# The last attention layer of a graph network: one-hot products from rows kept on chip in place of a scatter, with its output blocks issued by SyncE

## The reference

```python
h = (x @ W).reshape(n, H, C)                       # H = 2 heads of C = 64
a_s = einsum('nhc,hc->nh', h, att_src); a_d = einsum('nhc,hc->nh', h, att_dst)
e = leaky_relu(a_s[s] + a_d[d], 0.2)               # s, d: the edges, then a loop for each node
p = exp(e - segment_max(e, d)[d])
alpha = p / (segment_sum(p, d)[d] + 1e-16)
out = segment_sum(h[s] * alpha[:, :, None], d) + b
h_out = out + x @ Wsk2 + bsk2                      # then the outer residual and layernorm
```

## Time and profile before

| what | us |
|---|---|
| median of 3 runs | 6690.39 (6684.87 to 6695.83) |
| span of the profiled execution | 5389.4 |
| what lies around the span (median less span) | 1301.0 |
| the stages from the first instruction of e4g to the end | about 897 |

### The profile page before, as it was taken

The page is one execution under the profiler, slowest core; times in us unless marked ns, Lnnn a source line. Parts: engine busy times, 40 slices in busy tenths (PEclk is TensorE's granted clock), DMA queues, the critical chain, the costliest instruction groups (busy, mean ns, idle before and its releaser), DMA issues. The chain is left out here.

```text
span 5389.4 us, 98297 instructions
## 1 busy us (share of the span) xinstructions
PE 3527.9 (65%) x21061; PEld 2451.3 (45%) x21062; DVE 3341.7 (62%) x13740; ACT 2224.4 (41%) x6490; POOL 3612.4 (67%) x4923
## 2 busy tenths in 40 slices
PE   4447798777688699969599999520009994100398
PEld 3437687767566344412166666410007773100133
DVE  6454587444388576778488888623518886153388
ACT  0015476767577344423278888300004441000155
POOL 2767577767545677637488888675755556757698
PEclk8669999999899899979799999755559996555699
DMA  1015598989999611101134444341129985311498
GB/s 43 1 56 159 173 281 249 264 245 262 216 279 278 245 53 53 46 17 38 51 124 141 142 142 142 115 122 34 41 81 291 290 290 159 83 32 41 153 343 299
DMA packets 574488, 817.78 MB, mean 152 GB/s; under 512 B 143654, under 2 KB 291021, under 8 KB 573858
## 3 DMA queue, kind: packets, MB, share of 16 engines
q1 hardware_dynamic: 419372, 557.29, 33.3%
q0 software_dynamic: 69184, 122.90, 9.2%
q10 hardware_dynamic: 85784, 136.02, 6.7%
HBM read 494.99 MB, written 329.46 MB: 153 GB/s over the span
## 5 line engine op out<-in xcount | busy, mean ns | idle before, releaser
L619 POOL DMA_INDIRECT agg_dst<-e_rows,e_put_i x392 | 390.6, 996 | 204.3 <-issue 118.8
L1889 POOL DMA_INDIRECT e_rows<-h,e_other_i x392 | 389.2, 993 | 150.9 <-issue 118.9
L1219 POOL TENSOR_TENSOR n_rstd<-n_rstd,minus_half 128x4 f32<-128x4 f32 x294 | 333.5, 1134 | 23.1
L688 POOL DMA_INDIRECT agg<-e_msg,e_put_i x196 | 195.0, 995 | 166.3 <-DVEq L717 115.0
L1232 ACT ACTIVATE n_o<-n_y_ps,n_shift,n_rstd 128x128 f32<-128x128 f32 x784 | 293.6, 458 | 14.8 <-POOL n_shift L1502 13.7
L365 POOL DMA_INDIRECT by_src<-s_pay_s,s_place_i x196 | 189.1, 965 | 114.0 <-issue 58.9
L2388 POOL TENSOR_TENSOR n_u<-n_u 128x512 f32<-128x512 f32 x98 | 124.5, 1271 | 205.8 <-DVE n_u L2335 205.8
L905 POOL DMA_INDIRECT x_rows<-x,d_other_i x196 | 185.8, 948 | 86.1 <-issue 58.8
L2189 PE MATMUL n_y_ps<-n_w,n_gt 128*128 128x128 f32 x1568 | 240.4, 276 | 0.0
L1712 POOL DMA_INDIRECT lg_rows<-x,e_other_i x196 | 186.4, 951 | 78.0 <-issue 59.4
L1113 PE MATMUL e_xl_ps<-gat_wl,e_xg 128*128 128x512 f32 x392 | 225.1, 657 | 18.0 <-ACT e_xg L1086 18.0
(11 more groups left out here) (510 smaller groups left out, 11771.4 us busy)
## 6 DMA issues: line engine op xcount, KB each, us to landing
n_ag<-agg_dst SPq DMA_DIRECT2D x294, 264.0 KB, 3.9
n_hs<-h SPq DMA_DIRECT2D x196, 264.0 KB
n_xs<-x SPq DMA_DIRECT2D x196, 256.0 KB, 4.3
agg_dst<-e_ev SPq DMA_DIRECT2D x196, 132.0 KB
y<-n_o ACTq DMA_DIRECT2D x98, 264.0 KB, 3.6
e1a_fed<-y SPq DMA_DIRECT2D x196, 132.0 KB
m<-e1a_ev SPq DMA_DIRECT2D x196, 132.0 KB
e1b_fed<-m SPq DMA_DIRECT2D x196, 132.0 KB
```

The lines of the kernel that those rows point to most:

```text
L619: pool.indirect_dma_start(out=agg, out_offset=bass.IndirectOffsetOnAxis(ap=e.put_i[:, c:c + 1], axis=0), in_=rows[:, c, :], in_offset=None ...
L688: pool.indirect_dma_start(out=agg, out_offset=bass.IndirectOffsetOnAxis(ap=e.put_i[:, c:c + 1], axis=0), in_=msg[:, g % SLOTS, k, 0:out_wi ...
L1219: st(pool.tensor_tensor(rstd, rstd, keep.minus_half[:, :], ALU.pow))
L1889: pool.indirect_dma_start(out=rows[:, c, :], out_offset=None, in_=h, in_offset=bass.IndirectOffsetOnAxis(ap=e.other_i[:, c:c + 1], axis=0))\
```

## The change

Only the last attention layer changes; the one before it (`e3`, `n3`) keeps its form. `a4` now holds `a_s` and `a_d` (four values for each node), `s4` is 132 wide with ones in the last four columns, and the tables of `walk_tables` are kept to the end. `gat_edges` and `node_last` give way to `edge_shares` and `walk_last`.

`edge_shares` gathers as before, while TensorE and VectorE find four values of each edge's target (its own logit for two heads, and `a_d` for two). The gathered `a_s` is then added by TensorE, in edge order. `softmax` includes the self loop for each edge, and makes for each edge its final share and, for the last edge of a target, the target's own share less one. These go through HBM into edge order; the own share replaces columns 128 and 129 of the edge's row. There is no scatter and no `agg_dst`.

`walk_last` multiplies the rows by their shares (VectorE, 49 operations), and then walks the 396 steps; GpSimd makes the one-hot matrices. A block's two tiles start from `s4` (ScalarE), columns 0 to 127 collect the result and columns 128 and 129 the own share. When a block's steps are done (`close`, on SyncE), VectorE multiplies `h4` by the own share, adds the sums and takes the statistics; ScalarE takes the root and applies the norm, SyncE stores. SyncE issues all loads and stores.

```diff
-                        act.activation(ao[:, s, 2 * j:2 * j + 2, :], h_ps[j][:, :, D + GAT_HEADS:ROW], ACT.Copy).then_inc(h_kept[s], 1)
+                        act.activation(ao[:, s, 2 * j:2 * j + 2, :], h_ps[j][:, :, D:ROW], ACT.Copy).then_inc(h_kept[s], 1)
...
+def edge_shares(nc, keep, name, e, on_dst, krel_rows, h, a_nodes, values_edges, shares_edges, rows, share):
...
+                    pool.sem_inc(landed, 1)
...
+                    for turn in range(2):
+                        dve.wait_ge(node_ready, turn + 1)
+                        for half in range(2):
+                            of = banks[:, 4 + 2 * half:6 + 2 * half, 0:STEPS]
+                            to = [parts[:, :, half, part, 2 * turn:2 * turn + 2].rearrange("p s a -> p a s") for part in range(3)]
+                            link(dve.tensor_copy(to[0], of))
+                            link(dve.tensor_tensor(rest[:, :, :], of, to[0], ALU.subtract))
+                            link(dve.tensor_copy(to[1], rest[:, :, :]))
+                            link(dve.tensor_tensor(rest[:, :, :], rest[:, :, :], to[1], ALU.subtract))
+                            link(dve.tensor_copy(to[2], rest[:, :, :]))
...
+                            for half in range(2):
+                                for part in range(3):
+                                    ins = pe.matmul(banks[:, i // per_bank, col:col + values], hot[:, n % 2, half, k * P:(k + 1) * P],
+                                                    parts[:, i, half, part, :], start=(half, part) == (0, 0), stop=(half, part) == (1, 2))
...
+                    for v in range(values - 1, -1, -1):
+                        if v == GAT_HEADS - 1:
+                            ins.then_inc(summed, 1)
+                            pe.wait_ge(landed, 1)
+                        for half in range(2):
+                            to = banks[0:EQ, v // 2, (v % 2 * 2 + half) * P:(v % 2 * 2 + half + 1) * P]
+                            for b, (_, n) in enumerate(STEP_BLOCKS):
+                                ins = pe.matmul(to, on_dst.chunk_hot[0:n, b, half, :], turned[0:n, v, b, :], start=b == 0,
+                                                stop=b == len(STEP_BLOCKS) - 1 and v >= GAT_HEADS)
+                            if v < GAT_HEADS:
+
+                                ins = pe.matmul(to, rows[:, half::2, D + v], keep.ident[:, :], start=False, stop=True)
+                    ins.then_inc(summed, 1)
...
+                    sp.dma_start(shares_edges.rearrange("a (p j) -> p a j", p=P), out[:, :, :]).then_inc(stored, 16)
+                    sp.wait_ge(stored, 16)
+                    sp.dma_start(back[:, :, :], shares_edges.rearrange("a (q r) -> q a r", q=EQ)).then_inc(loaded, 16)
...
+def walk_last(nc, keep, e, rows, share, s4, h4, out):
...
+                for i in range(STEPS):
+                    if i % STEPB == 0:
+                        pool.wait_ge(steps_done, i + STEPB)
+                    ins = pool.tensor_scalar(hot[:, i // STEPB % HOTS, i % STEPB, :], keep.node_of[:, :], e.krel[:, i:i + 1], None,
+                                             ALU.is_equal)
...
+                def load(turn, s):
+                    upto(sp, owned, turn, s, SLOT)
+                    sp.dma_start(rows_of(hs, s), pair_rows(h4, turn, s)).then_inc(h_in[s % SLOT], 16)
+                    upto(sp, begun, turn, s, SLOT, 2)
+                    sp.dma_start(rows_of(ss, s), pair_rows(s4, turn, s)).then_inc(s_in[s % SLOT], 16)
...
+                def store(turn, s):
+                    upto(sp, normed, turn, s)
+                    sp.dma_start(pair_rows(out, turn, s), rows_of(r, s)).then_inc(stored[s % SLOT], 16)
+
+                run(sp, (0, load), (4, close), (7, store))
...
+                def begin(turn, s):
+
+                    upto(act, added, turn, s, OPEN_BLOCKS)
+                    act.wait_ge(s_in[s % SLOT], (use_of(turn, s) + 1) * 16)
+                    act.activation(sums(s)[:, :, 0:ROW], ss[:, s % SLOT, :, :], ACT.Copy).then_inc(begun, 2)
...
+                run(act, (0, begin), (PAST, begin_past), (5, take_root), (6, apply))
...
+                run(dve, (2, scale), (1, statistics), (2, move), (0, weigh), (1, mean_and_variance), (0, add))
...
-        gat_edges(nc, keep, "e4", to_dst, on_dst, krel_rows, h4, a4, a_edges, agg_dst)
-        node_last(nc, keep, s4, h4, agg_dst, out)
+        with nc.sbuf_tensor("h_rows", [P, J, ROW], F32) as rows, nc.sbuf_tensor("share", [P, GAT_HEADS, J], F32) as share:
+            edge_shares(nc, keep, "e4", to_dst, on_dst, krel_rows, h4, a4, values_edges, shares_edges, rows, share)
+            walk_last(nc, keep, on_dst, rows, share, s4, h4, out)
```

More of the change, by code:

```diff
@@ L446, in edge_tables @@
         e.split = sb("split", [P, 1])
+        e.last = sb("last", [P, J])
     def lay_out(block, more, banks):
@@ L451, in lay_out @@
         after, before = ph.sb("after", [P, 1]), ph.sb("before", [P, 1])
-        tmp, end = ph.sb("tmp", [P, J]), ph.sb("end", [P, J])
+        tmp, end = ph.sb("tmp", [P, J]), e.last if full else ph.sb("end", [P, J])
         diag, off = ph.sb("diag", [P, 2, P]), ph.sb("off", [P, P])
@@ L2480, in _ @@
                     done(act, h_out, last_turn(s), s, 32)
[L2483 to L2493, removed]
-        with nc.Block() as block:
+SHARES = 2 * GAT_HEADS
@@ L2495, in _ @@
             @block.sync
             def _(sp):
[L2497 to L2530, removed]
+                ends = []
@@ new lines, in add, with after_store, statistics @@
+                def add(turn, s):
+                    after_store(dve, turn, s)
+                    upto(dve, owned, turn, s)
+                    dve.tensor_tensor(r[:, s % SLOT], u[:, s % 2], sums(s)[:, :, 0:D], ALU.add).then_inc(added, 1)
+                def after_store(dve, turn, s):
+                    n = use_of(turn, s) * 16
+                    if not isinstance(n, int) or n > 0:
+                        dve.wait_ge(stored[s % SLOT], n)
+                def statistics(turn, s):
+                    upto(dve, added, turn, s)
+                    for g in range(GB):
+                        ins = dve.bn_stats(stats[:, s % 2, g, :], r[:, s % SLOT, g, :])
+                    ins.then_inc(taken, 1)
@@ new lines, in mean_and_variance, with scale, move @@
+                def mean_and_variance(turn, s):
+                    upto(dve, taken, turn, s)
+                    dve.sem_inc(go, 1)
+                    for g in range(GB):
+                        ins = dve.bn_aggr(mv[:, s % SLOT, g, :], stats[:, s % 2, g, :])
+                    ins.then_inc(together, 1)
+                def scale(turn, s):
+                    upto(dve, rooted, turn, s)
+                    dve.reciprocal(rstd[:, s % SLOT, :], root[:, s % SLOT, :]).then_inc(scaled, 1)
+                def move(turn, s):
+                    upto(dve, scaled, turn, s)
+                    dve.scalar_tensor_tensor(shift[:, s % SLOT, :], mv[:, s % SLOT, :, 0], -1.0, rstd[:, s % SLOT, :], ALU.mult, ALU.mult)\
+                        .then_inc(shifted, 1)
```

299 lines of the change are left out of this document (268 added, 31 removed).

## The result

The changed kernel takes 6524.12 us (median of 4 runs, 6516.96 to 6543.28), the kernel before 6689.96 in the same session: a ratio of 0.9756, 95% interval 0.9739 to 0.9773, or 166 us less. The forecast was 6530. Its total was right; three of its terms were 11 to 23 us off, and their errors cancelled.

The account below looks back on a forecast made before the run. It took GpSimd's gathers to bound e4g, its scatters e4m, and DMA transfers n4. Terms 7 + 8 + 15 - 279 + 89 = -160 us gave span 5229 and, with 1301 us carried over, 6530 us, range 6455 to 6620.

Parts of the forecast that it names:

- The 1301 us between it and the median are carried over: Whole kernel: 1301.0 us between the profiled span of 5389 us and the median stay unchanged, their nature unknown.
- e4g under the gathers, +7: e4g: extra slice work stays hidden under the gathers; casts on VectorE hold up gathers, +7 us (0 to 9).
- e4g, the tail, +8: End of e4g: 20 products waiting for `landed`, a copy, a store and a load add 8 us, or 17.
- e4s, +15: e4s: more VectorE operations, a store, a load and 8 transposes add 15 us, bounds 11 to 20.
- e4m, -279: e4m: the whole scatter stretch goes but for about 1 us of barrier, -279 us.
- n3, 0: n3: larger `s4` and `a4` stores are covered by TensorE's products, 0 us, bound 5.
- n4, 42 us before the first block: Start of n4: VectorE multiplies all rows in 33.6 us, plus 8 for sharing a port with GpSimd.
- n4, 98 x 3.7: n4: 98 blocks at 3.7 us each, 363 us; with start and end 413 against 324, +89 us.
- the ring: n4: after each add VectorE rests 0.9 us for ScalarE's begin and root, making a block 3.7 us.
- VectorE bound, no ring: Rival for n4: ScalarE runs ahead and loads land early, block 3.0 to 3.1 us, 6466 us; chance 0.15.
- The load ring: n4: SyncE's `s4` load waits behind a store, 3.05 to 4.15 us a block; load or clock rival 0.20.
- GpSimd's comparison decides: Rival for n4: one-hot matrices above 0.9 us each set the block, kernel slower; chance 0.10, of which 0.04 slower.

Follow-up runs that it names:

- second profile of before: The kernel before, unchanged, profiled again beside timed executions: 6706.96 us, ratio 1.0004, span 6709.2 us.
- e_three: Changed kernel with half-width one-hot comparisons (half of the nodes get no edges), reciprocal and store each one round later: 6425.74 us, ratio 0.9600.
- e_spread: Changed kernel with reciprocal one round later and row weighings spread, 8 groups in front, then one every second round: 6498.86 us, ratio 0.9713.
- v_b: Changed kernel with late reciprocal and store, spread row weighings, two parts per product in e4g, 66 one-hot matrices on VectorE: 6445.85 us, ratio 0.9628.
- e_gathers_late: Changed kernel, but in e4g GpSimd starts its 196 gathers only when all 66 slices are done: 6562.16 us, ratio 0.9802.

## Why the prediction came out right, step by step

- **"The 1301 us between it and the median are carried over"**: the number served, its place was wrong. They are in the stages in which GpSimd issues indirect DMAs; the time around the span is 2 us. Since the gathers of e4g are in both kernels, the error mostly cancelled in the difference; it did not in the next two points.
- **e4g under the gathers, +7**: the holding up of gathers by casts was right: from first to last gather's start 258.9 us after, 250.6 before, +8.3. The failed step is "It costs nothing as long as that cover of about 55 us holds". There is no cover: beside gathers TensorE issues a product in 2.8 us, so most slices come behind them, and from the last gather to the last slice are 100.0 us after against 81.9 before: +18.1.
- **e4g, the tail, +8**: from the last slice to the first logit 36.1 after, 24.1 before: +12.0, of which the edge-order products are the main reason (from 8.9 to 19.4 us, with the sums of `a_s` among them) and not the wait for `landed`, which was counted long before. The term's premise, that `a_dst` was on chip long before the last gather, did not hold in these executions: before, its store stands at 6062.34, 100 us behind the last gather. Store to load took 3.1 us, not 2.4.
- **e4s, +15**: +13.9. The stage as a whole was sized well; store to load took 2.9 and load to transposes 3.3, where 2.4 each were put.
- **e4m, -279**: the stage is gone; in this second profile of before it had 290.1, 10 more than in the first.
- **n3, 0**: from its first instruction to e4g 478.3 us after, 478.7 before.
- **n4, 42 us before the first block**: 38.5, from the first load to `weigh` at 6156.18. VectorE's rows took 29.6 of them (33.6 put), and 8.9 came behind (8 put). The place of the 8 was other than I thought: not VectorE but GpSimd was held up. Its first comparison (not the second, as an expectation above has it) took 26.68 us, the five others of the first batch came after it, and TensorE's first product at 6153.07 was released by them.
- **n4, 98 x 3.7**: 3.60, and the ring of add, begin, root and reciprocal is as written, 0.94 us of rest. Two sizes in this sum were off. "I take 0.5" for the comparison: 0.913, above the point of 0.9 from which, as the prediction said, GpSimd decides. And "VectorE 3.0": e_three shows 0.955 x 2.605 = 2.5 us busy, because neighbouring operations overlap (in the changed kernel they sum to 3.6 us a block and cover 2.6). With a late reciprocal alone (GpSimd) 3.60, with a half comparison alone (ring) 3.53, with both (SyncE's load behind a store, inside my 3.05 to 4.15) 3.43: three limits within 5%. The forecast named two and priced them right. The third, GpSimd, was put at 2.0 and came out at the same place, which is luck: 100 us of the window hold 112 comparisons, one in 0.89 us, which is 3.61 for 4.04 of them. A comparison of 1.2 us would have left the ring as it is and made a block of 4.8 us.
- **The rivals**: "VectorE bound, no ring" did not happen; in e_three, where VectorE is 96% and DMA 99% busy, a block is 2.6 and not 3.0. The load ring is real and hidden behind the two others. TensorE did not stay at 1.2 GHz in n4: the mean granted clock was 0.88 with TensorE two thirds busy, and 0.98 once the block was 2.6 us. "GpSimd's comparison decides" was given 0.10, and it is half true: an equal partner of the ring, 0.5 us from costing the gain (the prediction's break-even was 1.42 for a matrix).
- **Its own signs**: the root as releaser (94.6 us), the begin right behind the add and the DMA share (0.73) came as written. Two of the three signs of being wrong came too: the comparison is above 0.9 us, and the time around the span changed, from 1301 us to 2. So the total came out right partly by luck; what the runs bear out is the ring, its size, and the stage that is gone.

Why an execution of the kernel before could run its gathers with TensorE at full pace, while every other one profiled here could not, was not found. That instructions come late beside gathers with nothing outstanding that the profile shows is read from the timeline: TensorE's in the changed kernel's e4g, VectorE's in that of the kernel before, where in lg too VectorE waits 204 us in line 1791 for "issue". What holds them up was not tested.

## What to carry to other kernels

When two engines wait for each other and a third is full, take the waits one at a time and then together: here the late reciprocal alone gained nothing, the half comparison alone 9 us of n4, the two together 17, and with the late store all three 97. A profile's span far below the measured time means that it is not the execution to plan on; before work is put under another engine's time, look whether it really ran there in such an execution. An engine that seems idle enough for "one cheap operation" is to be priced by the operation, not by the engine's share of busy time.

## What the runs showed of the hardware

- GpSimd's comparison with a value for each partition took 0.913 us on 256 elements and 0.600 on 128: 2.4 ns for an element of a partition and 0.29 us besides (an estimate, from a line through the two). A two-input product of 512 elements took 1.05, so the comparison costs more for an element than the product.
- The Trainium skill, "GPSIMD Engine Reference", section "Performance versus the Vector engine", puts a good one-input loop at about 1.8 cycles an element, 1.5 ns. An estimate by that page is 0.38 us for the matrix; the measured 0.913 decides.
- One comparison that began while VectorE ran 49 two-input operations end to end was over only when those were: 26.68 us from 6121.42, the last of them starting at 6146.6. The Trainium skill, "SBUF — State Buffer", section "Who interferes with whom", calls the shared port an exclusive lock; the trace agrees, and shows that a comparison need not get its turn between two instructions of a series. With the series broken up (e_spread) the longest was 2.04 us.
- VectorE's own comparison of the same 256 elements took 0.35 to 0.58 us beside GpSimd (median 0.398, in v_b).
- Beside indirect gathers TensorE issued 82 products in 180 us (changed kernel), without them 2376 in 81 us (e_gathers_late). One execution, that of the earlier trace rows, ran 792 products in 77 us beside gathers.
